# Second attention of a four-layer block: one mask product fewer on PE, two small steps more on DVE

## The reference

```python
H, dh = 16, 8
q, k, v = split_heads(query @ wq_k + wq_b), split_heads(key_in @ wk_k + wk_b), split_heads(...)
logits = einsum('bhqd,bhkd->bhqk', q, k) / sqrt(dh)
neg = (1.0 - mask) * -1000000000.0
logits = logits + neg[:, None, :, :]
attn = softmax(logits, axis=-1) * group_prob[:, None, :, :]
out = einsum('bhqk,bhkd->bhqd', attn, v) @ wo_k + wo_b
```

## Time and profile before

| | |
|---|---|
| Median of 3 runs | 828.68 us (827.31 to 829.53) |
| The profiled execution's own time | 829.18 us |
| Its span in the profile | 827.4 us |
| PE busy | 662.5 us, 80% |
| DVE busy | 639.3 us, 77% |
| ACT busy | 363.7 us, 44% |
| POOL busy | 357.8 us, 43% |
| Second attention, its rows and loop | from 359 to 445 us of the span |

### The profile page before, as it was taken

How to read it: one execution, slowest core, us unless ns; L and a number is a source line. 1 busy time by engine, 2 the same in 40 slices (tenths; PEclk the granted TensorE clock), 3 DMA queues, 4 the chain that set the end, 5 groups by cost and what they waited for, 6 DMA issues and landing times.

```text
span 827.4 us, 17071 instructions
## 1 busy us (share of the span) xinstructions
PE 662.5 (80%) x5144; PEld 317.1 (38%) x5144; DVE 639.3 (77%) x1199; ACT 363.7 (44%) x630; POOL 357.8 (43%) x642
## 2 busy tenths in 40 slices
PE   1359924999988684878993899999999976997696
PEld 0113312444434463324542344444444432454342
DVE  5558764799977786666886799999999967575696
ACT  1314411888875441332331445555555545333443
POOL 6065624577742155205665244554444420025251
PEclk9755555999997798689996899999999988899799
DMA  8000000121204000000000111111111100000110
GB/s 257 0 0 2 0 0 8 44 55 53 55 27 124 2 3 2 1 0 2 2 2 11 33 53 51 52 55 55 53 50 53 55 13 1 2 3 2 32 54 29
DMA packets 46244, 26.81 MB, mean 32 GB/s; under 512 B 17255, under 2 KB 45207, under 8 KB 46032
## 3 DMA queue, kind: packets, MB, share of 16 engines
q1 hardware_dynamic: 44792, 24.36, 10.6%
q10 hardware_dynamic: 1408, 1.85, 0.6%
HBM read 25.63 MB, written 0.56 MB: 32 GB/s over the span
## 4 chain that ended last, share of the span: by engine, by line
PE 64%; DVE 20%; POOL 8%; issue 6%; ACT 2%; DVEq 0%; POOLq 0%; ACTq 0%
PE PS L187 51%; PE PS L446 4%; POOL RSTD L302 4%; DVE SHARED L875 3%; DVE MB L909 2%; PE PS L997 2%; PE PS L888 2%; PE PS L1003 1%; DVE MF L909 1%; POOL VE L300 1%; DVE STAT L290 1%; DVE REC L1011 1%; PE PS L962 1%; DVE XN L306 1%; PE PS L940 1%
## 5 line engine op out<-in xcount | busy, mean ns | idle before, releaser
L709 ACT ACTIVATE SHARED<-SHARED 128x512 f16<-128x512 f32 x180 | 112.4, 630 | 126.8 <-DVE SHARED L724 122.3
L729 DVE TENSOR_TENSOR SHARED<-SHARED 128x512 f16<-128x512 f32 x180 | 145.8, 830 | 12.6 <-ACT SHARED L709 12.2
L724 DVE TENSOR_TENSOR SHARED<-SHARED,PS 128x512 f32<-128x512 f32 x180 | 120.9, 686 | 11.3 <-ACT SHARED L702 7.3
L187 PE MATMUL PS<-XH,UH 128*128 128x512 f16 x296 | 113.9, 385 | 2.2 <-ACT CT L553 2.2
L187 PE MATMUL PS<-XL,UH 128*128 128x512 f16 x296 | 113.8, 384 | 0.0
L187 PE MATMUL PS<-XH,UL 128*128 128x512 f16 x296 | 113.7, 384 | 0.0
L187 PE MATMUL PS<-SHARED,DNH 128*128 128x512 f16 x360 | 107.1, 379 | 5.4 <-DVE SHARED L729 5.3
L980 ACT ACTIVATE SHARED<-PS 128x512 f32<-128x512 f32 x96 | 52.3, 595 | 99.2 <-PE PS L187 74.2
L720 DVE TENSOR_TENSOR SHARED<-SHARED,PS 128x512 f32<-128x512 f32 x116 | 78.7, 679 | 10.7 <-PE PS L187 10.7
L656 POOL CAST DNH<-DF 128x128 f16<-128x128 f32 x90 | 26.0, 289 | 134.6 <-PE PS L187 134.6
L646 POOL TENSOR_TENSOR UL<-UF,UH 128x256 f16<-128x256 f32 (+1 forms) x90 | 69.4, 771 | 7.2
(11 more groups left out here) (260 smaller groups left out, 1248.6 us busy)
## 6 DMA issues: line engine op xcount, KB each, us to landing
UF<-in_up SPq DMA_DIRECT2D x58, 128.0 KB, 2.0
DF<-in_down SPq DMA_DIRECT2D x90, 64.0 KB, 1.8
SEL<-in_sel SPq DMA_DIRECT2D x90, 32.0 KB, 1.7
UF<-in_up SPq DMA_DIRECT2D x32, 64.0 KB, 1.7
SHARED<-t_values_dram SPq DMA_DIRECT2D x2, 1024.0 KB, 10.5
SHARED<-in_masks ACTq DMA_DIRECT2D x1, 1024.0 KB, 10.3
WF<-in_wsmall SPq DMA_DIRECT2D x1, 868.0 KB, 6.2
X<-in_x SPq DMA_DIRECT2D x1, 512.0 KB, 3.7
```

The costliest lines, as they stand in the source:

```text
L187: last = pe.matmul(dst, l, r, start=start and i == 0, stop=stop and i == len(pairs) - 1)
L709: act.activation(HHI[:, u, hf, :], HF[:, hf, :], ACT.Copy).then_inc(sem("e_high"), 1)
L724: dve.tensor_tensor(HF[:, hf, :], src[:, hf, :], bank(4 + hf), ALU.mult).then_inc(sem("e_hidden"), 1)
L729: dve.tensor_tensor(HLO[:, u, hf, :], HF[:, hf, :], HHI[:, u, hf, :], ALU.subtract).then_inc(sem("e_low"), 1)
```

## The change

In `att_rows` of the second attention the product with `DGL` is left out. So a masked score has 61024 x 16384 = 999,817,216 taken off instead of 1e9. For a query with at least one key that is not masked, the maximum is the same. For a query whose keys are all masked, the negated maximum is now too small by 11.15625 x 16384 = 182,784. `att_max_split` puts that right with two new operations ahead of the five. The first writes 182,784 into `MF[:, 1]` where the negated maximum is over 5e8, and 0 elsewhere. The second adds that to `MF[:, 0]`. The counters of the semaphore go from 5 to 7 a batch. `att_cols` keeps both products.

```diff
 def att_rows(pe, a, b, p):
                 if a == 1:
-                    products(pe, bank(j % 2), [(d[:], over(NMA[:, b, :], 4)) for d in (DGH, DGL)], start=False)\
+                    products(pe, bank(j % 2), [(DGH[:], over(NMA[:, b, :], 4))], start=False)\
                         .then_inc(sem("a_rows"), 1)
 def att_max_split(dve, a, b, u):
-            s = lambda k: 5 * b + k
+            s = lambda k: 7 * b + k
             dve.wait_ge(sem("a_max"), 4 * (NB + b) + 4)
+            dve.tensor_scalar(MF[:, 1, :], MF[:, 0, :], 5e8, -MASK_LO * MASK_UNIT, ALU.is_gt, ALU.mult).then_inc(sem("a_msplit"), 1)
+            dve.wait_ge(sem("a_msplit"), s(1))
+            dve.tensor_tensor(MF[:, 0, :], MF[:, 0, :], MF[:, 1, :], ALU.add).then_inc(sem("a_msplit"), 1)
+            dve.wait_ge(sem("a_msplit"), s(2))
             dve.tensor_scalar(mb[:, :, :, 24], mf[0], 1.0 / MAX_UNITS[0], None, ALU.mult).then_inc(sem("a_msplit"), 1)
...
 def att_max_pe(pe, a, b, u):
             if a == 1:
-                pe.wait_ge(sem("a_msplit"), 5 * b + 5)
+                pe.wait_ge(sem("a_msplit"), 7 * b + 7)
```

More of the change, by code:

```diff
@@ L916, in att_max_split @@
             mf = [MF[:, i, :].rearrange("p (j g) -> p j g", j=4) for i in range(3)]
-            s = lambda k: 5 * b + k
+            s = lambda k: 7 * b + k
             dve.wait_ge(sem("a_max"), 4 * (NB + b) + 4)
+            dve.tensor_scalar(MF[:, 1, :], MF[:, 0, :], 5e8, -MASK_LO * MASK_UNIT, ALU.is_gt, ALU.mult).then_inc(sem("a_msplit"), 1)
+            dve.wait_ge(sem("a_msplit"), s(1))
+            dve.tensor_tensor(MF[:, 0, :], MF[:, 0, :], MF[:, 1, :], ALU.add).then_inc(sem("a_msplit"), 1)
+            dve.wait_ge(sem("a_msplit"), s(2))
             dve.tensor_scalar(mb[:, :, :, 24], mf[0], 1.0 / MAX_UNITS[0], None, ALU.mult).then_inc(sem("a_msplit"), 1)
-            dve.wait_ge(sem("a_msplit"), s(1))
+            dve.wait_ge(sem("a_msplit"), s(3))
             dve.scalar_tensor_tensor(mf[1], mb[:, :, :, 24], -MAX_UNITS[0], mf[0], ALU.mult, ALU.add).then_inc(sem("a_msplit"), 1)
-            dve.wait_ge(sem("a_msplit"), s(2))
+            dve.wait_ge(sem("a_msplit"), s(4))
             dve.tensor_scalar(mb[:, :, :, 25], mf[1], 1.0 / MAX_UNITS[1], None, ALU.mult).then_inc(sem("a_msplit"), 1)
-            dve.wait_ge(sem("a_msplit"), s(3))
+            dve.wait_ge(sem("a_msplit"), s(5))
             dve.scalar_tensor_tensor(mf[2], mb[:, :, :, 25], -MAX_UNITS[1], mf[1], ALU.mult, ALU.add).then_inc(sem("a_msplit"), 1)
-            dve.wait_ge(sem("a_msplit"), s(4))
+            dve.wait_ge(sem("a_msplit"), s(6))
             dve.tensor_copy(mb[:, :, :, 26], mf[2]).then_inc(sem("a_msplit"), 1)
```

## The result

The changed kernel takes 852.36 us (median of 5 runs, 850.14 to 854.62), against 829.41 us before (827.31 to 829.57, 5 runs in all). The ratio is 1.0284, with a 95% interval of 1.0263 to 1.0305: slower by 23 us. The forecast was 845.5 us in a range of 832 to 852. The direction and the mechanism were right. The time lies 0.4 us above the range.

The account below looks back on a forecast made before the run. No single engine was taken as the bound (PE busy 80%, DVE 77%), so the changed stage was read by itself. 829.18 + 9.8 for holds + 7 for low clock = 846.0 us profiled, 845.5 as median, range 832 to 852.

Parts of the forecast that it names:

- The holds: In the split on DVE, steps meeting a running POOL pair wait for a POOL operation; max_pe 2.47 us later in iteration 1.
- The two steps that it named: Old L923 and L925 in the split, each held for one POOL operation of 1.25 us by POOL's second pair.
- max_pe at R + 6.33: R is the start of rows(b+1, 1) on PE; in iterations 3 to 5 max_pe was to come 6.33 us after it.
- The sum of the holds: Second attention, all iterations: 2 x 2.04 + 3 x 1.76 + 1.46 - 1.0 = +9.8 us.
- The start: Batch 0 and iteration 0 of the second attention: shorter blocks and an earlier chain of batch 1, together -1.0 us.
- the 0.36 us of pause ahead of the transpose: Iterations 3 to 5: PE issues nothing in the last 0.36 of the 3.16 us from max_pe to the transpose.
- The clock: PE's waits of some 3.1 us in iterations 1 to 6 bring the low clock: 8.4 us in all, taken as +7.
- one in six be spared: One of the six iterations 1 to 6 may escape the low clock, so 8.4 us becomes +7.
- Holds without the low clock: Rival: DVE's split steps are held, but PE's low clock mostly does not come; 839 us, chance 0.21.
- Only one step is held: Rival: in the split L923 slips in ahead of POOL's pair and the CAST is not held; 831.5 us, chance 0.11.
- The short steps keep POOL back: Rival: the split's chain goes through once started and POOL's pair waits for it; 829 us, no change, chance 0.08.
- Faster: Rival: the new steps hide in the 0.40 us that L919 waits for POOL's first pair; 825 us, chance 0.05.

Follow-up runs that it names:

- the PE half: Against the kernel before, only the product with DGL is gone from the rows and the split keeps its five steps: 832.5 us, ratio 1.0029.
- PE kept busy: The changed kernel with 11 needless products on PE between cols(b, 1) and max_pe(b+1): 842.3 us, ratio 1.0158 to the kernel before.

## Why the prediction came out as it did

**The holds: right, and their size right.** The prediction put the start of POOL's second pair 3.53 us behind the iteration's start, and it was measured at 3.52. The two steps that it named were held, for 1.27 and 1.16 us. max_pe at R + 6.33 was forecast and measured. With the clock kept up, the periods were 9.83, 10.12 and 10.38, against 9.84, 10.12 and 10.33. The Trainium skill's rule (GPSIMD Engine Reference, Key points), by which POOL contends with DVE instructions in a 2-port mode or with two SBUF inputs, agrees with the traces: L921, with two inputs in SBUF, took 1.26 us in batch 1. The CAST took 1.24 in the PE half. The runs add the length: the hold lasted to the end of a POOL operation, and with one operand in PSUM there was none. The prediction's own sentence was too wide, though: it had every DVE operation on SBUF alone held while POOL runs a pair. The statistics L290 read `X` in SBUF, and in the kernel before they took 0.29 us inside a pair, as long as anywhere else in this attention (0.29 to 0.30):

```profile
393.97 2.50 POOL L984 TENSOR_TENSOR SHARED<-SHARED,GPT 128x512 f32<-128x512 f32 x2 [1.11 <-ACT SHARED L980]
395.60 0.29 DVE L290 BATCH_NORM_STATS2 STAT<-X 128x6 f32<-128x128 f32 x1
```

**The sum of the holds: 9.8 forecast, 10.6 measured.** PE kept busy leaves +9.1. That run also spares the low clock of iteration 0. It cost 1.5 us in the changed kernel (11.02 less 9.54); taking the same for the kernel before, where it was there too, the holds alone are 10.6, an estimate. Two smaller readings were off as well. The start was to gain 1.0 us and gained 0.7 by the same estimate, and the 0.36 us of pause ahead of the transpose stand in no row (the earlier trace rows have 0.18), which with a period of 10.38 for 10.33 us made no difference.

**The clock: the term that failed, 7 forecast, 9.4 measured.** The rest of the 10.9 us, 1.5, is the low clock of iteration 0, there before the change too. I took 1.6 us for a wait from iteration 0 and let one in six be spared. The mechanism held, but a low stretch after the change mostly costs more. Iterations 1, 3, 4 and 5 lost 2.8, 3.0, 1.3 and 2.4 us against the run with PE kept busy (12.60 less 9.83 for the first), and iteration 6 with what follows lost 2.5. Together that is 11.9 us, where the forecast had 6.8 for these five. In iteration 1 PE worked 6.3 us at 0.50. In the kernel before, the 4.26 us of work that I had priced ran at 0.60 on average, and the clock was back at 1.00 behind them. Why it stayed low for longer now is open. And a low stretch gives something back, 2.5 us in iteration 2, which I had not seen. On POOL and on DVE of the changed kernel, iteration 2:

```profile
396.42 2.49 POOL L988 TENSOR_TENSOR SHARED<-SHARED,GPT 128x512 f32<-128x512 f32 x2 [6.51 <-ACT SHARED L984]
```

```profile
398.68 0.27 DVE L919 TENSOR_SCALAR MF<-MF 128x16 f32<-128x16 f32 x1
```

The columns of iteration 1 were slow, so the first pair started ahead of the rows at 396.50, not 0.35 us behind them. The compare was free at R + 2.45 instead of R + 2.88, and the chain got through before the second pair. Iteration 2 took 7.63 us, less than before. Taking one stretch's price as fixed, and the iterations as alike, is the step that failed.

**Outside the attention: 3.1 us, with no term.** The range had been drawn from the cases of the attention alone. That these 3.1 us are the change's is not shown: the time outside goes from 741 to 749 us over the twelve kernels, more than the 6.9 us between forecast and measurement. So the profiled execution came 6.3 us above its 846.0 by 0.8 of the holds, 2.4 of the clock and 3.1 from outside, and the median half a microsecond more, since the execution profiled after the change did not stand above its median. Had any one of the three been right, the time would have lain inside the range, so that it lies just outside is in part chance; that the clock's term was a quarter too small is not.

**The rivals.** "Holds without the low clock" (839) is what the run with PE kept busy shows, at 842.3 us. The holds came, and the low clock with them, as a second half of the cost. "Only one step is held" needed a CAST that is not held; it is. "The short steps keep POOL back" did not happen by itself (the pair took 2.48 us), but made to happen it gives 826.5 us, near the 829 worked out, though that is in part luck: iteration 0 got 3.8 us shorter, where the sum had 1.0 for the whole start. "Faster", the new steps hidden in the first wait, fell with L919 at 0.80 us.

## What to carry to other kernels

Before putting small DVE operations into a chain, lay POOL's operations beside them in time: an operation of the kinds held here (a TENSOR_SCALAR or a CAST from SBUF to SBUF, or an operation with two inputs in SBUF) that meets a running POOL operation waits until that ends, however small it is, and saving work elsewhere can bring the two together. Look for the hold in the durations, since no list of waits names it: the same form with two durations. The ways out are operands in PSUM, another order, or one wait that keeps POOL behind the chain. A wait of PE that grows, by 3 us here and in some iterations by only 1.5, is to be priced with the lower clock that may follow it, and by a range: one low stretch cost 1.3 to 3.0 us in the same loop.

## What the runs showed of the hardware

- A 128x16 operation on DVE took 0.17 to 0.20 us alone in SBUF, 0.17 to 0.23 us with an operand in PSUM, and up to 1.31 us in SBUF beside POOL's 128x512 multiply (the CAST of iteration 5 in the PE half). POOL's pairs took 2.48 to 2.51 us in these loops, with held operations beside them and without, so POOL paid nothing.
- A held operation gets in between two POOL operations that follow each other without a gap (L927 and L929 above, one each), so two dependent steps were held one after the other. The gap can be missed: the norm of the kernel before, at 411.78, came 0.09 us ahead of it (410.62 + 1.25) and was held through the second operation too, 1.42 us in all.
- Adding 77 products to PE made the kernel 10 us faster, since the granted clock over the attention rose from 0.78 to 0.93.
